# Expert columns head-innermost, choice and product in one VectorE instruction, mean of squares on GpSimd

## The chip, the core and the metric

The kernel runs on one core of a Trainium2 chip. The core has five engines that run side by side, each with its own queue in program order: TensorE (PE; PEld is its loading of weights), VectorE (DVE), ScalarE (ACT), GpSimd (POOL) and SyncE (SP), which issues DMAs here. They are held together by semaphores. The metric is the device time of one execution in microseconds, and lower is better.

## What is computed

`x` has 2 x 1024 tokens of 512 columns. After a layer norm, two attentions are computed and added to `x`.

The first ("local") has 16 query heads and 4 key/value heads of 32 columns, with biases, a norm over the 32 columns of each head and a rotary embedding; a query sees 64 keys back. The norm divides by the root of the mean of squares:

```python
rms = jnp.sqrt(jnp.mean(x * x, axis=-1, keepdims=True) + RMS_EPS)
```

The second ("routed") has 16 query heads, but one key and one value per token, chosen by a gate among 16 experts:

```python
gating = jax.nn.softmax(x @ W_gate.T, axis=-1)
idx = jnp.argmax(gating, axis=-1)
indicator = jax.nn.one_hot(idx, H, dtype=gating.dtype)
top1_val = jnp.max(gating, axis=-1, keepdims=True)
q, k, v = jnp.split(x @ W_qkv.T, 3, axis=-1)
k_shared = jnp.einsum('bth,bthd->btd', indicator, k)
v_shared = jnp.einsum('bth,bthd->btd', indicator * top1_val, v)
```

Attention over them is causal over 1024 tokens.

## The kernel before, in words

A planner (`make_plan`) writes one list of steps before the program is built, from costs and due times that it holds for each step; every engine's program walks this same list, so the order of each queue is fixed by hand. The change touches neither the planner nor its costs.

The first stage runs in 8 rounds of 256 tokens, two tiles of 128 each (`a` = 0, 1). In a round TensorE multiplies the normalised and transposed tokens with the weights, in parts: `kvg` (local key and value, and the gate's 16 columns), `q`, `fk` and `fv` (all 16 experts' keys and values, 512 columns each), and `qt` (routed queries, transposed, four chunks). Each float32 product is made of three matmuls of high and low halves. The results go to two PSUM banks in turn (`gemm`), and TensorE may use a bank again when VectorE or ScalarE has read it (`gemm_read`). The local attention of the tile before, its output projection and the first row maxima of the routed attention (`first_max`, L1292 and L1299, into `r_first`) are woven in between. All transposes but those of the probabilities go through one more bank, `tp1`. The second stage is the rest of the routed attention, eight units over k_stack and v_all.

The steps that the change touches, for one tile:

- `kv_biased` (L1172 to L1180) adds the bias and takes the gate's maximum; `g_score` is the rank where the gate equals its maximum, and 0 elsewhere. `gate_sum` takes the greatest rank (`g_rank`, L1186) and marks it (`g_hot`, L1188).
- `picked` (L1211) multiplies the 16 experts' columns, in the bank, by `g_hot`; this frees the bank. The sum over the heads (L1216) gives `chosen`, 32 columns. In the bank and in `picked` the columns lie head after head, 32 each.
- `fk_hi` (ScalarE, L1437 and L1439) copies the chosen key, rounded for the matmul, into two parts of `fk_stack[a]`, the high half twice; `fk_lo` (VectorE, L1223) makes the low half, `chosen - high`, in the third. `fk_stack` (TensorE, L965) transposes both tiles' stacks through `tp1`, and ScalarE (L1481) copies them to `k_stack`. `fv_out` (L1428) scales the chosen value.
- `qt` (ScalarE L1460, VectorE L1249) makes the high and low halves of a chunk of routed queries.
- `q_square` (ScalarE L1449) squares queries and keys of the local attention; `q_rms` sums each head's 32 squares on VectorE (`rms_t`, L1238), divides by 32 and adds epsilon there (`rms_v`, L1242), and GpSimd raises to the power -1/2 (`rms_y`, L1610). GpSimd's rotary work (L1634, L1640, L1644) goes before it, and its product with `rms_y` (L1618) after it; then TensorE transposes the queries (L949).

## Time and profile before

| | |
|---|---|
| timed runs, median of 3 | 686.83 us (685.67 to 688.93) |
| profiled execution, span | 684.4 us |
| profiled execution, its own time | not listed; the timed runs are other executions |
| TensorE busy | 646.0 us, 94% of the span |
| VectorE busy | 496.3 us, 73% |
| ScalarE busy | 362.5 us, 53% |
| GpSimd busy | 442.6 us, 65% |

The span goes from the first to the last instruction of one execution. Busy time is the time in which an engine worked on at least one instruction.

### The profile page before, as it was taken

To read this page: it belongs to the slowest core of one execution; us is meant where nothing else is said; L and a number is where in the kernel's file an instruction comes from. 1 tells how busy PE (TensorE), PEld (TensorE's weight loads), DVE (VectorE), ACT (ScalarE), POOL (GpSimd) and SP (SyncE) were. 2 spreads that over 40 slices of the span, in tenths; PEclk is the share of its full clock that TensorE was granted. 3 is DMA by queue.
4 is the path that set the end of the run, shared out by engine and by line. 5 is a ranking of instruction groups with operands and counts; after the bars stand their busy time and mean duration, and the time that the engine had idled before them with its cause. 6 is when DMAs were issued, how large, how long until landed. Compare 5 with 4: busy or idle time off the path is not lost.

```text
span 684.4 us, 19451 instructions
## 1 busy us (share of the span) xinstructions
PE 646.0 (94%) x7432; PEld 510.2 (75%) x7432; DVE 496.3 (73%) x1328; ACT 362.5 (53%) x906; POOL 442.6 (65%) x368
## 2 busy tenths in 40 slices
PE   3788999999999899999899899999999999999997
PEld 3577888887788688888688667777777777777775
DVE  3956966677678866787676368888888787879454
ACT  4436444472527344445335555556566566656674
POOL 3965764938195735684487267685868777778730
PEclk9979999999999999999999999999999999999999
DMA  8522213231232032222214541321314131402011
GB/s 295 206 59 86 82 38 115 86 98 51 66 102 61 30 112 70 64 70 74 77 32 118 158 142 56 96 64 50 111 49 110 51 106 32 110 28 87 4 33 33
DMA packets 64942, 56.61 MB, mean 83 GB/s; under 512 B 6481, under 2 KB 48849, under 8 KB 64849
## 3 DMA queue, kind: packets, MB, share of 16 engines
q1 hardware_dynamic: 62704, 54.45, 27.2%
q8 instruction: 58, 0.95, 0.6%
q10 hardware_dynamic: 2144, 0.93, 0.5%
q14 instruction: 36, 0.29, 0.1%
HBM read 37.20 MB, written 17.89 MB: 80 GB/s over the span
## 4 chain that ended last, share of the span: by engine, by line
PE 78%; DVE 9%; POOL 4%; ACT 3%; issue 2%; DMA 2%; ACTq 1%; DVEq 0%; POOLq 0%
PE gemm L938 17%; PE s_ps L1047 12%; PE od_ps L1096 11%; PE st_ps L1080 10%; PE gemm L1024 6%; PE od_ps L1110 5%; PE win L998 3%; PE gemm L934 3%; PE win L983 2%; PE s_ps L1119 2%; DMA rope_t<-rope 2%; PE av L1010 2%; DVE l_sum L1266 2%; ACT p_loc L1492 2%; DVE l_max L1257 1%
## 5 line engine op out<-in xcount | busy, mean ns | idle before, releaser
L938 PE MATMUL gemm<-w_tok,xt 128*128 128x512 f32 (+1 forms) x768 | 186.1, 384 | 3.3 <-DVE x_res L1283 0.9
L938 PEld LDWEIGHTS gemm<-w_tok,xt 128*128 128x128 f32 x768 | 131.7, 193 | 28.2 <-issue 1.4
L1318 DVE CUSTOM_DVE_ANT_0 s_ps<-s_ps,x_ln 128x512 f32<-128x512 f32 (+3 forms) x224 | 127.6, 620 | 24.4 <-PE s_ps L1047 24.0
L1047 PE MATMUL s_ps<-k_stack,w_tok 96*128 96x512 f32 (+2 forms) x336 | 101.5, 385 | 0.3 <-DVE x_res L1283 0.3
L1080 PE MATMUL st_ps<-w_tok,k_stack 98*128 98x512 f32 x288 | 99.0, 413 | 0.2 <-ACT p_loc L1540 0.2
L1540 ACT ACTIVATE p_loc<-st_ps 128x512 f32<-128x512 f32 x144 | 77.7, 599 | 36.0 <-PE st_ps L1080 34.8
L1634 POOL TENSOR_TENSOR rope_b<-qkv,sin_t 128x128 f32<-128x128 f32 (+1 forms) x32 | 27.5, 880 | 79.5 <-DVE qkv L1232 79.3
L1047 PEld LDWEIGHTS s_ps<-k_stack,w_tok 96*128 96x128 f32 x336 | 55.0, 188 | 28.3 <-DVE picked_fk L1318 12.4
L1492 ACT ACTIVATE p_loc<-win,l_max 128x96 f32<-128x96 f32 x256 | 60.9, 391 | 19.1 <-DVE l_max L1257 19.0
L934 PE MATMUL gemm<-xt,w_qt 128*128 128x256 f32 x384 | 57.1, 293 | 6.3 <-DVE picked_fv L1211 3.5
L1540 ACT ACTIVATE p_loc_t<-st_ps 128x512 f32<-128x512 f32 x96 | 52.4, 599 | 19.8 <-PE st_ps L1080 19.3
L1318 DVE CUSTOM_DVE_ANT_0 s_ps<-s_ps,x_ln,picked_fk 128x128 f32<-128x128 f32 (+3 forms) x112 | 56.8, 556 | 7.5 <-PE s_ps L1047 7.1
L1658 POOL TENSOR_TENSOR p_loc<-p_loc,l_rec 128x1536 f32<-128x1536 f32 x16 | 44.1, 2757 | 26.9 <-DVE l_rec L1269 26.9
L1610 POOL TENSOR_TENSOR rms_y<-rms_v,minus_half 128x20 f32<-128x20 f32 x16 | 58.6, 3665 | 3.3 <-DVE rms_v L1242 2.8
L934 PEld LDWEIGHTS gemm<-xt,w_qt 128*128 128x128 f32 x384 | 50.6, 194 | 10.2 <-DVE picked_fv L1211 4.5
L1024 PE MATMUL gemm<-w_o,attn_t 128*128 128x512 f32 x192 | 54.8, 414 | 3.2 <-DVE attn_t L1274 2.4
L1080 PEld LDWEIGHTS st_ps<-w_tok,k_stack 98*128 98x128 f32 x288 | 50.5, 189 | 9.0 <-ACT p_loc L1540 2.1
L1318 DVE DVE_READ_ACCUMULATOR2_ANT picked_fk<- 128x1 f32 x336 | 47.8, 142 | 0.0
L1501 ACT ACTIVATE p_loc_t<-win 96x512 f32<-96x512 f32 x64 | 36.8, 634 | 16.6 <-PE win L998 16.5
L1096 PE MATMUL od_ps<-p_loc,v_all 128*32 128x128 f32 x1152 | 44.3, 277 | 0.0
L1024 PEld LDWEIGHTS gemm<-w_o,attn_t 128*128 128x128 f32 x192 | 34.1, 193 | 10.0 <-issue 3.2
L1676 POOL TENSOR_SCALAR_AFFINE_SELECT p_loc<-p_loc 128x512 f32<-128x512 f32 x40 | 25.0, 634 | 24.8 <-ACT p_loc L1540 24.8
(172 smaller groups left out, 1298.7 us busy)
## 6 DMA issues: line engine op xcount, KB each, us to landing
w_tok<-q_parts SPq DMA_DIRECT2D x72, 128.0 KB, 2.6
q_parts<-qt SPq DMA_DIRECT2D x120, 64.0 KB
x_ln<-x SPq DMA_DIRECT2D x8, 512.0 KB, 4.7
x_res<-x SPq DMA_DIRECT2D x16, 256.0 KB, 2.9
partial<-x_res SPq DMA_DIRECT2D x16, 256.0 KB, 2.6
w_tok<-partial SPq DMA_DIRECT2D x8, 512.0 KB, 5.2
raw<-w_tok SPq DMA_DIRECT2D x3, 1024.0 KB, 12.9
v_win<-v_rows SPq DMA_DIRECT2D x64, 48.0 KB, 2.2
```

Source lines behind the costliest of these rows:

```text
L934: i = e.matmul(g[:, 0:PAIR], w_qt_p[r][:, k, a * P:(a + 1) * P], xs[l][:, k, :], start=first, stop=last)
L938: i = e.matmul(g[:, 0:cols], xs[l][:, k, a * P:(a + 1) * P], w_tok_p[r][:, k, c0:c0 + cols], start=first, stop=last)
L1024: i = e.matmul(gemm[bank][:, :], attn_t[l][:, kc, :], w_o_p[r][:, kc, :], start=kc == 0 and q == 0, stop=kc == KC - 1 and q == 2)
L1047: e.matmul(s_ps[bank][:, 0:cols], q_op[b][0:HALVES, i, h, :], k_stack[0:HALVES, b * S + c0:b * S + c0 + cols], start=True, stop=True).then ...
L1080: e.matmul(st_ps[k % ST_BANKS][:, :, :], k_stack[0:HALVES + 2, b * S + j * P:b * S + (j + 1) * P], q_op[b][0:HALVES + 2, i, :, :], start=T ...
L1096: mm = e.matmul(od_ps[h * DK:(h + 1) * DK, 0, :], v_all[:, b * IT + j, 0:DK], p_t[k % RING][:, h, :], start=i == j, stop=ends_row(k))
L1318: e.tensor_tensor_reduce(out=s[:, 0:cols], in0=s[:, 0:cols], in1=causal[:, S - width + c0:S - width + c0 + cols], scale=1.0, scalar=dst if ...
L1492: i = e.activation(p_loc[a][:, g, quad, :], win[:, g, quad * KEYS:(quad + 1) * KEYS], ACT.Exp, bias=l_max[:, a, n:n + 1])
L1501: e.activation(p_loc_t[quad][0:KEYS, :, :].rearrange("p g q -> p (g q)"), win[0:KEYS, quad, :], ACT.Copy).then_inc(*M["p_t_r"].did((m, a, ...
L1540: e.activation(p_t[k % RING][:, :, :], st_ps[k % ST_BANKS][:, :, :], ACT.Exp, scale=ROUTED_SCALE).then_inc(*M["rp_exp"].did((u, k)))
L1610: e.tensor_tensor(rms_y[:, :], rms_v[:, :], minus_half[:, :].to_broadcast([P, NH]), ALU.pow).then_inc(*M["rms_r"].did((n, a)))
L1658: e.tensor_tensor(p_l, p_l, l_rec[:, a, :].unsqueeze(2).to_broadcast([P, H, KEYS]), ALU.mult).then_inc(*M["p_r"].did((m, a)))
```

## The change

The weights of the experts' keys and values are handed over with their columns ordered column-major over heads (all 16 heads of column 0, then of column 1, and so on), so that `picked` and its sum find the 16 heads of a column side by side. `g_hot` goes: one `scalar_tensor_tensor` compares the ranks with the greatest and multiplies the bank's columns by the outcome. The chosen key lies in the fourth part of `fk_stack[a]`; ScalarE's second copy has its sign turned, and the low half is a sum of two, `chosen + (-high)`, by `tensor_reduce`; the query's low half has its sign turned as well, so that their product stays. The division by 32 and the epsilon go from VectorE to GpSimd. The list of steps stays.

```diff
-    chosen = {k: sb(one, f"chosen_{k}", [P, DK]) for k in ("fk", "fv")}
-    fk_stack = [sb(one, f"fk_stack{a}", [P, HALVES]) for a in range(2)]
+    chosen_fv = sb(one, "chosen_fv", [P, DK])
+    fk_stack = [sb(one, f"fk_stack{a}", [P, HALVES + DK]) for a in range(2)]
+    chosen = {("fv", a): chosen_fv[:, :] for a in range(2)} | {
+        ("fk", a): fk_stack[a][:, HALVES:HALVES + DK] for a in range(2)}
...
-                e.tensor_reduce(g_rank[:, a:a + 1], g_score[:, a, :], AX.X, ALU.max).then_inc(*seq.did())
-                lane.wait_ge(*seq.now())
-                e.tensor_scalar(g_hot[:, a, :], g_score[:, a, :], g_rank[:, a:a + 1], None, ALU.is_equal).then_inc(
-                    *seq.did(("hot", n, a)))
+                e.tensor_reduce(g_rank[:, a:a + 1], g_score[:, a, :], AX.X, ALU.max).then_inc(*seq.did(("rank", n, a)))
...
-                e.tensor_tensor(picked[kind][:, :].rearrange("p (h d) -> p h d", h=H),
-                                g[:, :].rearrange("p (h d) -> p h d", h=H),
-                                g_hot[:, a, :].unsqueeze(2).to_broadcast([P, H, DK]), ALU.mult).then_inc(
-                                    *M["gemm_read"].did((n, kind, a)))
+                e.scalar_tensor_tensor(picked[kind][:, :].rearrange("p (d h) -> p d h", h=H),
+                                       g_score[:, a, :].unsqueeze(1).to_broadcast([P, DK, H]), g_rank[:, a:a + 1],
+                                       g[:, :].rearrange("p (d h) -> p d h", h=H), ALU.is_equal, ALU.mult).then_inc(
+                                           *M["gemm_read"].did((n, kind, a)))
                 lane.wait_ge(*M["gemm_read"].of((n, kind, a)))
-                e.tensor_reduce(chosen[kind][:, :], picked[kind][:, :].rearrange("p (h d) -> p d h", h=H), AX.X,
+                e.tensor_reduce(chosen[kind, a], picked[kind][:, :].rearrange("p (d h) -> p d h", h=H), AX.X,
                                 ALU.add).then_inc(*M[f"picked_{kind}"].did((n, a)))
...
-                lane.wait_ge(*M["fk_hi"].of((n, a)))
-                e.tensor_tensor(dst[:, 2 * DK:3 * DK].bitcast(F32R), chosen["fk"][:, :], dst[:, 0:DK],
-                                ALU.subtract).then_inc(*M["fk_lo"].did((n, a)))
+                lane.wait_ge(*M["fk_dup"].of((n, a)))
+                chosen_and_minus_hi = dst[:, DK:4 * DK].rearrange("p (b d) -> p d b", d=DK)[:, :, ::2]
+                e.tensor_reduce(dst[:, 2 * DK:3 * DK], chosen_and_minus_hi, AX.X,
+                                ALU.add).then_inc(*M["fk_lo"].did((n, a)))
...
-                e.tensor_reduce(rms_t[:, :], rope_sq[:, :, :], AX.X, ALU.add).then_inc(*seq.did(("squares", n, a)))
-                lane.wait_ge(*seq.now())
                 if n or a:
-                    lane.wait_ge(*M["rms_r"].of(tile_before(n, a)))
-                e.tensor_scalar(rms_v[:, :], rms_t[:, :], 1.0 / DK, RMS_EPS, ALU.mult, ALU.add).then_inc(
-                    *M["rms_v_r"].did((n, a)))
+                    lane.wait_ge(*M["rms_m_r"].of(tile_before(n, a)))
+                e.tensor_reduce(rms_t[:, :], rope_sq[:, :, :], AX.X, ALU.add).then_inc(*M["rms_v_r"].did((n, a)))
...
-                e.tensor_tensor(qt_of(1, n, c), g[:, 0:PAIR], qt_of(0, n, c).bitcast(F32),
+                e.tensor_tensor(qt_of(1, n, c), qt_of(0, n, c).bitcast(F32), g[:, 0:PAIR],
                                 ALU.subtract).then_inc(*M["gemm_read"].did((n, "qt", c)))
...
-                e.activation(dst[:, 0:DK].bitcast(F32R), chosen["fk"][:, :], ACT.Copy).then_inc(
-                    *M["fk_hi"].did((n, a)))
-                e.activation(dst[:, DK:2 * DK].bitcast(F32R), chosen["fk"][:, :], ACT.Copy).then_inc(
+                e.activation(dst[:, 0:DK].bitcast(F32R), chosen["fk", a], ACT.Copy).then_inc(*M["fk_hi"].did((n, a)))
+                e.activation(dst[:, DK:2 * DK].bitcast(F32R), chosen["fk", a], ACT.Copy, scale=-1.0).then_inc(
                     *M["fk_dup"].did((n, a)))
...
+                e.tensor_scalar(rms_v[:, :], rms_t[:, :], 1.0 / DK, RMS_EPS, ALU.mult, ALU.add).then_inc(
+                    *M["rms_m_r"].did((n, a)))
+                lane.wait_ge(*M["rms_m_r"].of((n, a)))
                 e.tensor_tensor(rms_y[:, :], rms_v[:, :], minus_half[:, :].to_broadcast([P, NH]), ALU.pow).then_inc(
                     *M["rms_r"].did((n, a)))
```

## Rows read from the trace of the kernel before

**Rows 1.** The page's first line.
```profile
span 684.4 us, 19451 instructions
```

**Rows 2.** Stretches: us, busy time of each engine, granted clock, DMA share, GB/s.
```profile
20.00:40.00 20.00, 13.71 (x66) 11.24 (x66) 17.58 (x27) 5.86 (x11) 18.42 (x11) 0.81 0.35 124
60.00:180.00 120.00, 119.15 (x1087) 100.09 (x1085) 85.98 (x176) 57.86 (x178) 74.63 (x53) 1.00 0.28 83
180.00:340.00 160.00, 151.93 (x1296) 127.01 (x1297) 120.20 (x225) 72.34 (x232) 98.81 (x69) 1.00 0.25 72
400.00:684.00 284.00, 278.69 (x4336) 204.83 (x4336) 220.05 (x826) 174.44 (x355) 196.58 (x186) 1.00 0.24 66
```

**Rows 3.** TensorE's waits, 0 to 400: us in total, times, longest.
```profile
PE tp L965 <- DVE fk_stack L1223: 4.0, 4, 1.8
PE gemm L934 <- DVE picked_fv L1211: 3.5, 4, 1.6
...
PE tp L949 <- POOL qkv L1618: 1.4, 2, 1.2
```

**Rows 4.** Groups on VectorE, 0 to 400: count, busy us, mean ns, idle before.
```profile
L1216 DVE TENSOR_REDUCE chosen_fk<-picked_fk 128x32 f32<-128x512 f32 x16 | 17.5, 1094 | 0.5
...
L1238 DVE TENSOR_REDUCE rms_t<-rope_sq 128x20 f32<-128x640 f32 x16 | 12.9, 807 | 2.7 <-ACT rope_sq L1449 2.7
L1249 DVE TENSOR_TENSOR qt<-gemm,qt 128x256 fp32r<-128x256 f32 x30 | 12.5, 415 | 7.1 <-ACT qt L1460 7.1
L1223 DVE TENSOR_TENSOR fk_stack<-chosen_fk,fk_stack 128x32 fp32r<-128x32 f32 x16 | 11.5, 719 | 0.0
...
L1211 DVE TENSOR_TENSOR picked_fk<-gemm,g_hot 128x512 f32<-128x512 f32 x16 | 11.0, 685 | 2.7 <-PE gemm L938 2.5
...
L1242 DVE TENSOR_SCALAR rms_v<-rms_t 128x20 f32<-128x20 f32 x16 | 9.8, 612 | 0.6
L1188 DVE TENSOR_SCALAR g_hot<-g_score,g_rank 128x16 f32<-128x16 f32 x16 | 8.0, 499 | 0.6
...
L1180 DVE TENSOR_SCALAR g_exp<-gemm,g_max 128x16 f32<-128x16 f32 x16 | 3.6, 225 | 0.0
```

**Rows 5.** Line 1223's instructions: shortest, median, longest in ns.
```profile
L1223 DVE TENSOR_TENSOR fk_stack<-chosen_fk,fk_stack x16: 128/194/2291, 34.1 to 362.1; 128x32 fp32r<-128x32 f32 x16
```

**Rows 6.** Timeline near 236: start, duration, instruction, idle before and its releaser.
```profile
235.64 2.75 POOL L1658 TENSOR_TENSOR p_loc<-p_loc,l_rec 128x1536 f32<-128x1536 f32 x1
...
236.25 2.19 DVE L1223 TENSOR_TENSOR fk_stack<-chosen_fk,fk_stack 128x32 fp32r<-128x32 f32 x1
...
238.50 0.42 PE L965 MATMUL tp<-idt,fk_stack 128*96 128x128 f32 x2 [1.79 <-DVE fk_stack L1223]
```

**Rows 7.** Timeline of TensorE, four instructions that it came to idle.
```profile
205.00 0.96 PE L938 MATMUL gemm<-w_tok,xt 128*128 128x512 f32 x3 [0.41 <-DVE picked_fk L1211]
...
306.48 0.96 PE L934 MATMUL gemm<-xt,w_qt 128*128 128x256 f32 x6 [0.49 <-DVE picked_fv L1211]
327.46 1.08 PE L1010 MATMUL av<-p_loc_t,v_win 96*32 96x128 f32 x32 [0.97 <-DVE r_first L1299]
332.62 0.42 PE L965 MATMUL tp<-idt,fk_stack 128*96 128x128 f32 x2 [1.47 <-DVE fk_stack L1223]
```

**Rows 8.** Timeline of VectorE, in the queue ahead of two of those.
```profile
201.59 1.10 DVE L1242 TENSOR_SCALAR rms_v<-rms_t 128x20 f32<-128x20 f32 x1
...
304.98 0.85 DVE L1223 TENSOR_TENSOR fk_stack<-chosen_fk,fk_stack 128x32 fp32r<-128x32 f32 x1
```

**Rows 9.** Two groups on GpSimd, 0 to 400.
```profile
L1610 POOL TENSOR_TENSOR rms_y<-rms_v,minus_half 128x20 f32<-128x20 f32 x16 | 58.6, 3665 | 3.3 <-DVE rms_v L1242 2.8
...
L1579 POOL TENSOR_TENSOR ln_b<-ln_t,ln_y 128x2 f32<-128x2 f32 x8 | 1.6, 195 | 0.6
```

**Rows 10.** Timeline of the start, VectorE and GpSimd.
```profile
31.15 3.00 DVE L1134 TENSOR_TENSOR w_o<-raw,w_o 128x2048 fp32r<-128x2048 f32 x1
...
31.96 5.59 POOL L1610 TENSOR_TENSOR rms_y<-rms_v,minus_half 128x20 f32<-128x20 f32 x1
```

More of the change, by code:

```diff
@@ L695 @@
 MARKS = (
-    "x_in xn_r ln_seq ln_b_r ln_v_r ln_y_r rms_v_r seq "
+    "x_in xn_r ln_seq ln_b_r ln_v_r ln_y_r rms_v_r rms_m_r seq "
     "xt_mm xt_hi xt_lo gemm_mm gemm_read kv_r sq_r rms_r rope_ab rope_sum rope_r "
@@ L771, in mixed_attention_kernel @@
     r_first = sb(one, "r_first", [P, IT, HQ])
-    g_exp, g_score, g_hot = (sb(one, n, [P, 2, H]) for n in ("g_exp", "g_score", "g_hot"))
+    g_exp, g_score = (sb(one, n, [P, 2, H]) for n in ("g_exp", "g_score"))
     over = ExitStack()
@@ L964, in tensor_program @@
                 for a in range(2):
-                    i = e.transpose(tp1[0:HALVES, a, :], fk_stack[a][:, :], idt[:, :])
+                    i = e.transpose(tp1[0:HALVES, a, :], fk_stack[a][:, 0:HALVES], idt[:, :])
                 i.then_inc(*M["fk_mm"].did(m))
@@ L1201, in vector_program @@
                 lane.wait_ge(*M["gemm_mm"].of((n, kind, a)))
-                lane.wait_ge(*seq.of(("hot", n, a)))
+                lane.wait_ge(*seq.of(("rank", n, a)))
                 if a or n:
@@ L1427, in scalar_program @@
                     lane.wait_ge(*filled_all())
-                e.activation(v_all[:, 2 * n + a:2 * n + a + 1, 0:DK], chosen["fv"][:, :].unsqueeze(1), ACT.Copy,
+                e.activation(v_all[:, 2 * n + a:2 * n + a + 1, 0:DK], chosen["fv", a].unsqueeze(1), ACT.Copy,
                              scale=g_top[:, a:a + 1]).then_inc(*M["fv_out"].did((n, a)))
@@ L1558, in seq_squares @@
     def seq_squares(n, a):
-        return M["seq"].of(("squares", *tile_before(n, a)))
+        return M["rms_v_r"].of(tile_before(n, a))
     def gpsimd_program(e):
@@ L1879, in heads, with by_column @@
         return w.reshape(-1, DK, *w.shape[1:])[:, even_first].reshape(w.shape)
+    def by_column(w):
+        return w.reshape(H, DK, D).swapaxes(0, 1).reshape(w.shape)
     def by_rep(w):
@@ L1888 @@
         "x": a["L0_attn_x"].reshape(TOK, D),
-        "w_tok": np.concatenate([wq, wk, a["L0_attn_Wv"], a["L0_ffn_W_gate"], fk, fv], 0).T,
+        "w_tok": np.concatenate([wq, wk, a["L0_attn_Wv"], a["L0_ffn_W_gate"], by_column(fk),
+                                 by_column(fv)], 0).T,
         "w_qt": fq.T,
```

## The prediction

> **What bounds the kernel now.** I read first how the span divides. The profiled execution spans 684.4 us [rows 1]; the three timed runs have a median of 686.83, 2.4 more, and since no time of the profiled execution itself is listed I make the sum on its span and carry the difference in microseconds over to the median. The stretches [rows 2] come next. TensorE is busy 119.15 of 120 us in 60 to 180 and 278.69 of 284 from 400 on, but 151.93 of 160 in 180 to 340 (8.07 idle), and 13.71 of 20 in 20 to 40. VectorE, where nearly all of the edit lies, is busy 86 of 120 and 120 of 160. So TensorE sets the pace; VectorE matters only where TensorE stands still for it. The edit touches the first stage alone, which ends near 400, so it can win no more than TensorE's idle time there.
>
> Second, whom TensorE waits for in that stage [rows 3]: 4.0 us in four stalls for the key's low half (L1223), 3.5 for the release of a bank by `picked_fv`, 1.4 in two stalls for the query tile that GpSimd scales last (L1618). Third, the groups of VectorE [rows 4] and the spread of one of them [rows 5]: the low half, 32 columns, has a median of 194 ns and a maximum of 2291. Fourth, why: at 236.25 it takes 2.19 us, and it ends, at 238.44, as GpSimd's 2.75 us `scaled` ends at 238.39; TensorE's transposes then start at 238.50 after 1.79 us idle [rows 6]. An instruction with two operands from SBUF was held until GpSimd's finished, and the profile counts the hold in its duration.
>
> **The change part by part.**
>
> *The sum over heads.* Now 1094 ns for 512 elements read 32 words apart [rows 4], 32 times (`fk` and `fv`). The other sum with neighbours side by side, `rms_t`, needs 807 ns for 640. Two VectorE products, 685 ns for 512 columns and 415 for 256, give 1.055 ns a column, so `rms_t` has 132 ns fixed, and a sum of 512 neighbours should take 132 + 540 = 672. Saved 0.42 us each, 13.4 us of VectorE in all. The bounds are 0 (if the 32 short results and not the distance are the cost) and 0.42. I take 0.42: `rms_t` has 20 results and shows no cost for them.
> The Trainium skill (Vector Engine (DVE) Microarchitecture Reference, 5.2 Measured stream behaviour on trn2) gives 0.65 cycle for each element that hops. By that rule the sum would save about 0.35 us, an estimate, and the whole forecast would be 0.2 us less. The row says 0.82 ns an element.
>
> *Choice and product in one.* It removes `g_hot`, 499 ns, 16 times: 8.0 us. The product keeps its 512 columns but takes a per-row scalar. `g_exp` has one and costs 225 ns for 16 columns, 208 fixed, where the plain product has 145 fixed. So 0.75 instead of 0.685, or 0.065 more, 32 times, 2.1 us. Bounds: 0.685 (the scalar is free) and 1.094 (the gate row that is read over and over walks like the strided sum). The row is 16 neighbours long, so I take 0.75. The bank comes free 0.065 later, counted from where the instruction starts.
>
> *Key's low half.* 719 ns on average now [rows 4]. As a sum of two over 32 pairs it has 64 elements: 132 + 68 ns, and 0.82 ns more for each hop, 52, so 0.25 us; bounds 0.13 (the least that the product took [rows 5] was 0.128) and 0.28. It has one source and should not be held. Saved 0.47 x 16 = 7.5 us. It now waits for the second ScalarE copy too, a copy of 32 columns behind the first; in the held cases both copies had long ended. The sign turned in the query's low half changes no count or shape.
>
> *Mean of squares to GpSimd.* VectorE loses 612 ns x 16 = 9.8 us. GpSimd gains an instruction on 20 columns between `rope`'s last sum and the power. The nearest row on GpSimd is `ln_b`, 195 ns for 2 columns [rows 9]; with 18 columns more and the wait for its own result I take 0.3 us, a guess between the bounds 0.2 (that row) and 0.61 (what the instruction took on VectorE), nearer to the first because the engine is the same. Where GpSimd stood waiting for VectorE's step it gets part of this back.
>
> VectorE sheds 13.4 + 8.0 + 7.5 + 9.8 - 2.1 = 36.6 us of busy time. Nearly all of it lies beside TensorE's work and is worth nothing. What counts are the stalls, one by one:
> - The low half's four stalls, 4.0 us [rows 3]: 1.79 at 238.50, 1.47 at 332.62 [rows 6, 7] vanish. Of the other two, 0.7 together, I count 0.5: they stand behind a queue of VectorE with shortened sums in it, not behind a hold. Sum 3.75.
> - `picked_fk` at 205.00, 0.41 [rows 7]: a held mean of squares, 1.10 us, stood in the queue before it [rows 8]; all goes. `picked_fv` at 306.48, 0.49: it started when a held low half, 0.85 us, ended [rows 8]; all goes. `r_first` at 327.46, 0.97: a strided sum of `fk` stands right in front; 0.42 goes. Sum 1.3.
> - Not gained: `x_res` and transposed `x` stalls, where VectorE had stood idle in front and only the longest reduction of local scores is in the way, and the stalls behind ScalarE.
> - The start. TensorE waits up to 1.2 us for the first query tile from GpSimd [rows 3], whose power took 5.59 us there because VectorE's weight subtraction, 3.00 us from 31.15, held it [rows 10]; the group's mean is 3.67 [rows 9]. VectorE gets there sooner, but the subtraction holds GpSimd just as long, now in the instruction before. So what TensorE waits for VectorE before that (the 1.6 us that is the longest of `picked_fv` [rows 3]) only moves behind, to the same wait for GpSimd, and the mean adds 0.35. The second stall for that result gets 0.3 longer. Cost 0.65.
>
> Sum: -3.75 - 1.3 + 0.65 = -4.4 us, to 680.0 in the span and 686.83 - 4.4 = 682.4 in the median.
>
> **The clock.** TensorE's granted clock is 0.81 of full in 20 to 40 [rows 2], so part of that stretch ran at the lower level (1.2 GHz), where TensorE was busy 13.71 of 20 us. Since the start keeps its idle time, only in another order, I leave it at nothing; the matmuls there can move by 2 us either way.
>
> **The rivals.**
> *A. The stalls are taken up by others.* TensorE arrives earlier at the transposes behind ScalarE's copies and at GpSimd's `rope`. For it: GpSimd's result came too late twice already [rows 3]. Against: that is 2 of 16 tiles. If only the two large low-half stalls go and half is given back: -1.6, 685.2.
> *B. More goes than I traced.* A VectorE queue 36.6 us shorter releases banks sooner everywhere. All of TensorE's 8.07 + 0.85 us idle in 60 to 340 gone [rows 2]: -9 us, 677.8. Against: several of these waits had VectorE idle before them.
> *C. GpSimd becomes the bound.* This ends slower. The mean is on the way to `q_t` in each of 16 tiles. If each paid 0.61 us and TensorE waited every time: -5.05 + 9.8 = +4.7, 691.6. It decides from 0.53 us a tile ((5.05 + 3.4) / 16). Against it: TensorE waited for this result only twice, 1.4 us in all [rows 3].
> The Trainium skill (GPSIMD Engine Reference, 8. Key points) says that elementwise work is about twice as fast on VectorE; by that alone the step would be dearer where it goes.
> *D. The fused product is slow.* At 1.09 us it eats the shortened sum, 0.41 x 32 = 13 us, and releases the bank later: four bank stalls grow by 0.34 more, two queues lose their shortened sum (0.25 and 0.42), and the result is -4.4 + 1.4 + 0.7 = -2.3, 684.5.
>
> **How the numbers follow.** Chances: forecast 0.55, A 0.20, B 0.15, C 0.06, D 0.04. No change that a measurement of this kernel can tell is within 0.5%, 3.4 us, so faster means under 683.4. My own case has 1 us to spare: three quarters of it are faster. Faster 0.42 + 0.15 = 0.57; same 0.13 + 0.20 + 0.04 = 0.37; slower 0.06. The range reaches to B below, 677.8, and above past A to 686.5, 0.3 us short of nothing gained at all. Outside lie C, half of B and the outer part of A: 0.06 + 0.08 + 0.05.
>
> **What the new profile would show.** `chosen` near 0.67 us, the fused `picked` near 0.75, the low half near 0.25 with no maximum over 0.4, no `g_hot`, a new GpSimd group under 0.3. VectorE busy near 460 us. In TensorE's waits the line for `fk_stack` nearly gone, L949 behind GpSimd near 2 us, and 180 to 340 with TensorE busy in all but about 3.5 us of its (shorter) stretch. Wrong would be: a new name at the head of TensorE's waits (A, C), a `picked` over 1 us (D), or a second spell at the lower clock outside the start and the end of the first stage.

## The result and the profile after

The changed kernel takes 680.69 us (median of 5, 680.16 to 682.2) against 686.72 for the kernel before (5 runs beside it): a ratio of 0.9919, 95% interval 0.9897 to 0.994. That is 6.0 us less, where 4.4 less was forecast, and the spans of the profiled executions say the same: 678.1 against 684.4 [rows 1]. The profiled execution's own time is 680.16.

The page's first lines, and the stretches of time: us, busy time of each engine with its count, granted clock, share of DMA, GB/s.

```profile
span 678.1 us, 19434 instructions
...
PE 641.4 (95%) x7432; PEld 508.8 (75%) x7432; DVE 461.8 (68%) x1296; ACT 362.7 (53%) x906; POOL 446.2 (66%) x384
```

```profile
20.00:40.00 20.00, 11.63 (x64) 9.04 (x63) 15.06 (x26) 6.19 (x11) 18.97 (x13) 0.99 0.41 137
40.00:60.00 20.00, 17.63 (x124) 15.08 (x124) 10.38 (x18) 9.95 (x31) 11.19 (x11) 0.84 0.14 38
60.00:180.00 120.00, 118.63 (x1085) 99.86 (x1084) 76.25 (x165) 58.48 (x179) 76.02 (x58) 1.00 0.27 83
180.00:340.00 160.00, 156.60 (x1337) 132.05 (x1336) 107.02 (x214) 77.46 (x248) 100.61 (x77) 1.00 0.25 75
340.00:400.00 60.00, 55.37 (x521) 44.73 (x522) 30.79 (x67) 30.67 (x84) 40.45 (x33) 1.00 0.46 125
```

The gain is where TensorE stood still before: 180 to 340 has 3.4 us without TensorE, where it had 8.07 [rows 2]. The start is not better. TensorE works 11.63 us of 20 to 40, not 13.71, though at a clock of 0.99 instead of 0.81, and the lower level (1.2 GHz) has moved behind it, to 40 to 60 at 0.84.

TensorE's waits from 0 to 400 (total, times, longest):

```profile
PE tp L951 <- POOL qkv L1617: 4.8, 2, 4.3
PE gemm L936 <- DVE picked_fv L1210: 3.9, 3, 2.4
...
PE av L1012 <- DVE r_first L1296: 0.7, 2, 0.6
```

TensorE waits for `fk_stack` nowhere in this stretch any more; before, that was 4.0 us in four stalls [rows 3]. The wait for GpSimd's query tile stands in its place, with 4.3 us at one stroke and 4.8 in all, where near 2 was forecast; the timelines below show that this is mostly the old wait at the start under another name.

Groups on VectorE and the two of GpSimd's power (count, busy us, mean ns, idle before), and the spread of the low half in ns:

```profile
L1210 DVE SCALAR_TENSOR_TENSOR picked_fk<-g_score,g_rank,gemm 128x512 f32<-128x512 f32 x16 | 11.9, 742 | 4.0 <-PE gemm L940 3.8
...
L1215 DVE TENSOR_REDUCE fk_stack<-picked_fk 128x32 f32<-128x512 f32 x16 | 11.0, 686 | 0.5
...
L1223 DVE TENSOR_REDUCE fk_stack<-fk_stack 128x32 f32<-128x64 f32 x16 | 3.3, 205 | 0.0
```

```profile
L1609 POOL TENSOR_TENSOR rms_y<-rms_v,minus_half 128x20 f32<-128x20 f32 x16 | 56.6, 3537 | 1.3
...
L1606 POOL TENSOR_SCALAR rms_v<-rms_t 128x20 f32<-128x20 f32 x16 | 3.3, 208 | 2.6 <-DVE rms_t L1240 1.5
```

```profile
L1223 DVE TENSOR_REDUCE fk_stack<-fk_stack x16: 160/212/217, 32.9 to 357.8; 128x32 f32<-128x64 f32 x16
```

Every price was met: the sum 686 ns (672 forecast), the fused product 742 (750), the low half 205 with a maximum of 217 (250, none over 400), the mean 208 (300). VectorE is busy 461.8 us (460 forecast).

The place of the first long stall, in the timeline of VectorE, GpSimd and TensorE:

```profile
237.01 0.21 DVE L1223 TENSOR_REDUCE fk_stack<-fk_stack 128x32 f32<-128x64 f32 x1
...
237.01 2.76 POOL L1657 TENSOR_TENSOR p_loc<-p_loc,l_rec 128x1536 f32<-128x1536 f32 x1
...
237.71 0.38 PE L967 MATMUL tp<-idt,fk_stack 128*96 128x128 f32 x2
```

GpSimd's long instruction runs as before, the low half takes 0.21 us beside it, and TensorE's transposes have no idle time in front [rows 6]. But look at the starts: both were issued at 237.01. Before, the low half came 0.61 us behind. At the second place (327.64 against 327.86) it is even ahead. So this trace does not tell whether the low half is fast because it has one source, or because it is no longer behind. That question led the experiments.

The start, on GpSimd and then TensorE:

```profile
30.88 3.55 POOL L1643 TENSOR_TENSOR qkv<-qkv,rope_b 128x640 f32<-128x640 f32 x1
34.51 0.21 POOL L1606 TENSOR_SCALAR rms_v<-rms_t 128x20 f32<-128x20 f32 x1
34.81 3.54 POOL L1609 TENSOR_TENSOR rms_y<-rms_v,minus_half 128x20 f32<-128x20 f32 x1
38.49 1.26 POOL L1617 TENSOR_TENSOR qkv<-qkv,rms_y 128x640 f32<-128x640 f32 x1
```

```profile
39.81 1.11 PE L951 MATMUL tp<-idt,qkv 128*128 128x128 f32 x4 [4.30 <-POOL qkv L1617]
...
56.66 1.01 PE L936 MATMUL gemm<-xt,w_qt 128*128 128x256 f32 x3 [2.37 <-DVE picked_fv L1210]
```

As forecast, the weights' subtraction (VectorE, 30.74 to 33.02) now holds `rope`'s last sum, 3.55 us here against a group mean of 1.69, instead of the power [rows 10]. The mean and its hand-off put 0.30 us (34.51 to 34.81) on the path to the first query tile.

Both programs issue the same 7432 matmuls in the same order, so one matmul's start can be compared with its own start in the other kernel. This shows where each microsecond went:

| matmul | before | after | after minus before |
|---|---|---|---|
| first query tile | 39.01 | 39.81 | +0.8 |
| behind `picked_fv` at the start | 56.00 | 56.66 | +0.7 |
| third query tile | 77.65 | 80.07 | +2.4 |
| behind `picked_fk` | 205.00 | 206.43 | +1.4 |
| first `fk_stack` place | 238.50 | 237.71 | -0.8 |
| behind `picked_fv` | 306.48 | 304.80 | -1.7 |
| first maxima | 327.46 | 324.82 | -2.6 |
| second `fk_stack` place | 332.62 | 328.36 | -4.3 |
| behind `attn_t`, near the end of the first stage | 386.13 | 381.86 | -4.3 |
| 5 us later | 390.84 | 384.95 | -5.9 |
| last round of the second stage | 666.18 | 659.86 | -6.3 |

### The profile page after: what moved, and what is told of

The parts are those of the page before. It is cut to its first block, busy times and chain, and to the rows that moved or that the text cites. A ratio compares the mean times of both kernels' runs of the same rounds, so it can differ in the third digit from the quotient of the medians.

```text
span 678.1 us, 19434 instructions
## 1 busy us (share of the span) xinstructions
PE 641.4 (95%) x7432; PEld 508.8 (75%) x7432; DVE 461.8 (68%) x1296; ACT 362.7 (53%) x906; POOL 446.2 (66%) x384
## 4 chain that ended last, share of the span: by engine, by line
PE 83%; POOL 5%; DVE 4%; ACT 3%; DMA 2%; issue 2%; ACTq 1%; DVEq 0%; POOLq 0%
PE gemm L940 19%; PE s_ps L1049 12%; PE od_ps L1098 11%; PE st_ps L1082 10%; PE gemm L1026 6%; PE od_ps L1112 5%; PE gemm L936 5%; PE win L1000 3%; PE win L985 3%; PE s_ps L1121 2%; DMA rope_t<-rope 2%; PE av L1012 2%; ACT p_loc L1488 2%; PE tp L951 1%; DVE l_max L1254 1%
## 5 line engine op out<-in xcount | busy, mean ns | idle before, releaser
L1609 POOL TENSOR_TENSOR rms_y<-rms_v,minus_half 128x20 f32<-128x20 f32 x16 | 56.6, 3537 | 1.3
```

The costliest lines, as they stand in the source:

```text
L1609: e.tensor_tensor(rms_y[:, :], rms_v[:, :], minus_half[:, :].to_broadcast([P, NH]), ALU.pow).then_inc(*M["rms_r"].did((n, a)))
```

## The experiments

Three sets, each on one chip beside runs of the kernel before. Ratios are to the kernel before of the same set, with 95% intervals. The diffs show the lines that matter; `...` marks what is left out.

**First set: what does each part give back when it is undone?** The low half with two sources again, everything else as in the changed kernel:

```diff
-                chosen_and_minus_hi = dst[:, DK:4 * DK].rearrange("p (b d) -> p d b", d=DK)[:, :, ::2]
-                e.tensor_reduce(dst[:, 2 * DK:3 * DK], chosen_and_minus_hi, AX.X,
+                e.tensor_tensor(dst[:, 2 * DK:3 * DK], dst[:, 3 * DK:4 * DK], dst[:, DK:2 * DK],
                                 ALU.add).then_inc(*M["fk_lo"].did((n, a)))
```

> The changed kernel, but the key's low half is again a product-type instruction with two operands from SBUF (chosen + minus high); same waits, layout and place. Theory H (holds: such an instruction is held while GpSimd works, and the few places where TensorE stands behind it are the gain): the longest comes back to 2 us or more, the stalls of TensorE at L965-type transposes come back with 3 to 4 us, median near 684.2. Rival P (proportional: each us of VectorE time shed gives the same 0.16 us, 5.6 of 34.5): VectorE gains about 8 us, so 1.3 us, median near 682.0.

Measured: 679.48 us, 0.9906 (0.9885 to 0.9927). Nothing was lost. The timeline at the place of the long stall (VectorE, GpSimd, TensorE):

```profile
235.10 0.18 DVE L1222 TENSOR_TENSOR fk_stack<-fk_stack 128x32 f32<-128x32 f32 x1
...
235.11 2.80 POOL L1656 TENSOR_TENSOR p_loc<-p_loc,l_rec 128x1536 f32<-128x1536 f32 x1
...
235.81 0.38 PE L967 MATMUL tp<-idt,fk_stack 128*96 128x128 f32 x2
```

The two-source instruction was issued 0.01 us ahead of GpSimd's and took 0.18. At the second place it came 0.21 ahead and took 0.30. Elsewhere it was still held, up to 1.52 us, but TensorE did not wait. (That it took 0.30 there is the tail of another instruction: GpSimd's product before it, L1616, ended at 326.02 and the low half at 326.06.) So in the changed kernel the form of the low half is worth nothing, and my reason for the gain seemed to fall.

The sum over heads strided again (expert columns head after head, and no reordering of the weights), the rest as changed:

```diff
-                e.tensor_reduce(chosen[kind, a], picked[kind][:, :].rearrange("p (d h) -> p d h", h=H), AX.X,
+                e.tensor_reduce(chosen[kind, a], picked[kind][:, :].rearrange("p (h d) -> p d h", h=H), AX.X,
...
```

> The changed kernel with the experts' columns head after head again: the fused product stays, the sum over heads walks 32 words apart. Theory H: the sum is back at 1.09 us, VectorE 13 us busier, but only the stalls with a shortened sum right in front come back (0.25 + 0.42 and a little), median near 681.6. Rival P: 13 x 0.16 = 2.1, median 682.8. If the distance is not what made it slow, the sum stays at 0.69.

Measured: 682.82 us, 0.9951 (0.9934 to 0.9969), against 0.9906 of the run above in the same set. The sum takes 1096 and 1084 ns again, and 3.3 us are lost against that run (the intervals are apart). That run differs in the low half's form too; against the changed kernel itself (0.9919) it is 2.2 us, with intervals that just overlap. The median is nearer to the rival's number (682.8) than to my sum (681.6).

The division and epsilon back on VectorE:

```diff
+                e.tensor_reduce(rms_t[:, :], rope_sq[:, :, :], AX.X, ALU.add).then_inc(*M["rms_v_r"].did((n, a)))
+                lane.wait_ge(*M["rms_v_r"].of((n, a)))
                 if n or a:
...
+                    lane.wait_ge(*M["rms_r"].of(tile_before(n, a)))
+                e.tensor_scalar(rms_v[:, :], rms_t[:, :], 1.0 / DK, RMS_EPS, ALU.mult, ALU.add).then_inc(
+                    *M["rms_m_r"].did((n, a)))
...
```

> The changed kernel with the division by 32 and the epsilon on VectorE again, as a tensor_scalar that can be held. Theory H: the 0.3 us on GpSimd's way to the first query tile and to that near 80 go (-0.6), the stall at picked_fk near 205 comes back (+0.4), median 680.5, within 0.5 of the changed kernel. Rival P: 9.8 us more VectorE, +1.6, 682.3. Rival C (GpSimd's way to the query tiles is the bound): 16 x 0.3 less, 4.8, median near 676.

Measured: 678.42 us, 0.9894 (0.987 to 0.9918): no slower than the changed kernel (680.5 was expected). The low half is issued 0.29 us behind GpSimd's instruction again and still takes 0.22:

```profile
235.19 2.76 POOL L1657 TENSOR_TENSOR p_loc<-p_loc,l_rec 128x1536 f32<-128x1536 f32 x1
...
235.48 0.22 DVE L1223 TENSOR_REDUCE fk_stack<-fk_stack 128x32 f32<-128x64 f32 x1
```

Being behind does not hold the one-source form.

The last subtraction of weights (`w_o`, 2.28 us on VectorE) done only when GpSimd has scaled the first query tile (`rope_r`):

```diff
+LATE_BEFORE = ("qt", 0, 1)
...
-            if step == "w_lo":
-                n, = key
+            if step == "w_lo" and key[0] == len(PIECES) - 1:
+                continue
+
+            if step == "w_lo" or (step, *key) == LATE_BEFORE:
+                n = key[0] if step == "w_lo" else len(PIECES) - 1
...
+                if step != "w_lo":
+                    lane.wait_ge(*M["rope_r"].of((0, 0)))
...
```

> The changed kernel with VectorE's last weight subtraction (2.3 us, two operands from SBUF) moved behind the first query tile's scaling on GpSimd, where GpSimd stands idle. Theory H: GpSimd's rotary sum there falls from 3.55 to 1.55 us, the first query tile comes 2.0 us sooner, and TensorE's stall of 4.3 us before it falls to about 2.3; median near 678.7. Rival S (the start is given back at the second tile, which waits for ScalarE's exponentials): the start's gain is eaten before 60 us, median 680.7.

Measured: 679.06 us, 0.9897 (0.9879 to 0.9916). GpSimd's sum takes 1.57 us instead of 3.55, and the first query tile's transposes start at 37.07 instead of 39.81, but only about 1.6 us is left in the total against the changed kernel, with intervals that overlap.

**Second set: each part alone on the kernel before.** The low half as a sum of two, with the two signs and the place of the chosen key that belong to it, and nothing else of the change:

```diff
-                lane.wait_ge(*M["fk_hi"].of((n, a)))
-                e.tensor_tensor(dst[:, 2 * DK:3 * DK].bitcast(F32R), chosen["fk"][:, :], dst[:, 0:DK],
-                                ALU.subtract).then_inc(*M["fk_lo"].did((n, a)))
+                lane.wait_ge(*M["fk_dup"].of((n, a)))
+                e.tensor_reduce(dst[:, 2 * DK:3 * DK], chosen_and_minus_hi, AX.X,
+                                ALU.add).then_inc(*M["fk_lo"].did((n, a)))
```

> The kernel before with only the key's low half changed to the sum of two (and the two signs turned, chosen key in the stack). Theory R (race for the port: the product form is held only where GpSimd's scaling of the local weights starts just before it; in the kernel before it does so twice with TensorE waiting behind): both long stalls go whole, 3.3 us, and 0.3 elsewhere; ratio 0.9948. Rival P (each us of VectorE time is worth 0.16 us): 8 us less, 1.3 us, ratio 0.998.

Measured: 680.13 us, 0.9911 (0.9891 to 0.9931). This one part alone measures as much as the whole change, and more than the 0.9948 that I expected, which lies outside the interval. Its low half is issued 0.56 us behind GpSimd's instruction, just where it was held before:

```profile
234.08 2.76 POOL L1660 TENSOR_TENSOR p_loc<-p_loc,l_rec 128x1536 f32<-128x1536 f32 x1
...
234.64 0.21 DVE L1226 TENSOR_REDUCE fk_stack<-fk_stack 128x32 f32<-128x64 f32 x1
...
234.93 0.40 PE L967 MATMUL tp<-idt,fk_stack 128*96 128x128 f32 x2
```

The shorter sum alone (columns head-innermost, two instructions for choice and product as before):

```diff
...
-                e.tensor_reduce(chosen[kind][:, :], picked[kind][:, :].rearrange("p (h d) -> p d h", h=H), AX.X,
+                e.tensor_reduce(chosen[kind][:, :], picked[kind][:, :].rearrange("p (d h) -> p d h", h=H), AX.X,
...
```

> The kernel before with only the experts' columns head-innermost: product with g_hot and sum, both with neighbours side by side. Theory R: the sum falls to 0.69; at the stall near 238 the low half is issued at about 235.84, still after GpSimd's scaling (235.64), so that hold stays; near 330 it comes within 0.1 us of it, either way; 1.0 us goes at other stalls. Together 1.0 to 2.5 us, ratio 0.9965 to 0.9985. Rival P: 13.4 x 0.16 = 2.1, ratio 0.997. What tells them apart is the low half's longest time near 238: over 2 us by R.

Measured: 685.57 us, 0.9997 (0.9981 to 1.0012). The sum is 686 ns, 0.41 less, 32 times, and none of it arrives in the time, though 1.0 to 2.5 us were expected. At the first long stall:

```profile
234.69 2.76 POOL L1658 TENSOR_TENSOR p_loc<-p_loc,l_rec 128x1536 f32<-128x1536 f32 x1
...
234.90 2.59 DVE L1223 TENSOR_TENSOR fk_stack<-chosen_fk,fk_stack 128x32 fp32r<-128x32 f32 x1
...
237.55 0.42 PE L965 MATMUL tp<-idt,fk_stack 128*96 128x128 f32 x2 [1.78 <-DVE fk_stack L1223]
```

The low half gets there 0.4 us sooner than before, 0.21 behind and not 0.61, and is held 0.4 us longer, 2.59 and not 2.19 [rows 6]. Held work ends when the holder ends; what is saved in front of it is spent in the hold. That is not the whole of it. Elsewhere this profile does gain: at 327 us its matmuls are 2.1 us ahead of the kernel before. The second long stall, 1.78 us and not 1.47, takes 0.4 of that, and the clock, which falls to the lower level 1.4 us behind this stall, takes 1.5.

Both the strided sum and the two-source low half put back into the changed kernel, so that the fused product and the mean on GpSimd are what is left of the change:

```diff
-                e.tensor_reduce(chosen[kind, a], picked[kind][:, :].rearrange("p (d h) -> p d h", h=H), AX.X,
+                e.tensor_reduce(chosen[kind, a], picked[kind][:, :].rearrange("p (h d) -> p d h", h=H), AX.X,
...
-                e.tensor_reduce(dst[:, 2 * DK:3 * DK], chosen_and_minus_hi, AX.X,
+                e.tensor_tensor(dst[:, 2 * DK:3 * DK], dst[:, 3 * DK:4 * DK], dst[:, DK:2 * DK],
...
```

> The changed kernel with both undone: the strided sum and the two-source low half. Undone singly, the low half cost nothing and the sum 2.2 us. Theory R: with the strided sum the low half is issued 0.2 to 0.4 us after GpSimd's scaling again, is held over 2 us near 240 and 330, and both TensorE stalls return: 3.5 us more than with the strided sum alone, ratio near 1.000. Rival P or plain addition: 0.9951, as with the strided sum alone, plus at most 1.3 us of VectorE's (0.997).

Measured: 688.33 us, 1.0034 (1.0019 to 1.0048). The low half is issued 0.41 us behind `scaled` and takes 2.39, and TensorE stands 2.00 us; at the second place it stands 1.74. Both times the clock falls behind the stall, at 241.28 and 336.85, and the matmuls lose 1.5 to 1.6 us more there; so more comes back than the 3.5 us expected.

The late weight subtraction together with the mean on VectorE (both diffs of the first set; shown here is GpSimd's side of the mean):

```diff
-                e.tensor_scalar(rms_v[:, :], rms_t[:, :], 1.0 / DK, RMS_EPS, ALU.mult, ALU.add).then_inc(
-                    *M["rms_m_r"].did((n, a)))
-                lane.wait_ge(*M["rms_m_r"].of((n, a)))
```

> The changed kernel with the last weight subtraction behind the first query tile's scaling, and the division by 32 back on VectorE. Theory: late subtraction gives 2.0 us at the start, the mean off GpSimd's way 0.6 there and at the third tile, and costs 0.4 near 205; against the kernel before a ratio of 0.987, 677.5. Rival S (the second tile waits for ScalarE's exponentials, which wait for the first query tile, so the start's gain stays; but the held mean comes back in the queue at 49 us): 0.990.

Measured: 676.21 us (4 runs), 0.9853 (0.9832 to 0.9875), the fastest of all. It is the changed kernel without its last part and with 2.28 us of VectorE moved out of GpSimd's way. The first query tile starts at 37.51.

**Third set: is it a race?** The first set had spoken against the low half and the second for it. A race would explain both: the two-source form is held only when it is issued behind GpSimd's `scaled`, and in the changed kernel the shorter sum and the mean on GpSimd together let it be first. This kernel is the changed one with the two-source low half, and the mean back on VectorE:

```diff
-                e.tensor_reduce(dst[:, 2 * DK:3 * DK], chosen_and_minus_hi, AX.X,
+                e.tensor_tensor(dst[:, 2 * DK:3 * DK], dst[:, 3 * DK:4 * DK], dst[:, DK:2 * DK],
...
+                e.tensor_scalar(rms_v[:, :], rms_t[:, :], 1.0 / DK, RMS_EPS, ALU.mult, ALU.add).then_inc(
+                    *M["rms_m_r"].did((n, a)))
```

> The changed kernel with the two-source low half and the mean of squares on VectorE; sum and fused product stay as changed. Undone singly, neither cost anything (0.991 and 0.989). Theory R: without the mean GpSimd's scaling starts 0.3 us sooner; with the mean on VectorE the low half came at 235.48 after the scaling at 235.19, and at 326.35 after 326.15, so the product form is held there over 2 us both times, and 3.3 us or more come back: ratio 0.994 to 0.998. Addition of the single results: 0.989 to 0.991.

Measured: 684.84 us, 0.9977 (0.9961 to 0.9994). Line 1222's spread and who waited, then the three instructions:

```profile
L1222 DVE TENSOR_TENSOR fk_stack<-fk_stack x16: 128/194/2608, 33.6 to 360.3; 128x32 f32<-128x32 f32 x16
...
  PE tp L967: 3.4, 2
```

```profile
234.58 2.75 POOL L1656 TENSOR_TENSOR p_loc<-p_loc,l_rec 128x1536 f32<-128x1536 f32 x1
...
234.86 2.52 DVE L1222 TENSOR_TENSOR fk_stack<-fk_stack 128x32 f32<-128x32 f32 x1
```

Both long stalls are back, 3.4 us in two. The same two-source form that lost nothing beside the mean on GpSimd loses 0.9977 - 0.9894 = 0.8% without it.

The mean alone on GpSimd, on the kernel before:

```diff
...
                     lane.wait_ge(*M["rope_r"].of(tile_before(n, a)))
+                e.tensor_scalar(rms_v[:, :], rms_t[:, :], 1.0 / DK, RMS_EPS, ALU.mult, ALU.add).then_inc(
+                    *M["rms_m_r"].did((n, a)))
+                lane.wait_ge(*M["rms_m_r"].of((n, a)))
```

> The kernel before with only the division by 32 and the epsilon on GpSimd. Theory R: GpSimd's scaling near 235.6 starts 0.3 us later, but the low half there came 0.6 us after it, so the hold and the stall stay, 0.3 us shorter; the start and the third tile pay 0.65; the stall at 205 goes. Sum -0.4 us, ratio 0.998 to 1.001. Rival P (9.8 us of VectorE at 0.16): 0.9977. Rival C (GpSimd's way is the bound, 0.3 a tile): +4.8 us, 1.007.

Measured: 688.11 us, 1.0033 (1.002 to 1.0047): slower, and outside the 0.998 to 1.001 expected. The low half comes 0.36 us behind (0.13 at the second place), so the race isn't won, and TensorE stands 2.04 and 1.85 us. The clock falls 1.4 us behind the first and 2.1 us behind the second. The windows (columns as above):

```profile
228.00:240.00 12.00, 9.87 (x76) 7.65 (x74) 9.85 (x15) 1.21 (x4) 11.47 (x8) 1.00 0.08 29
240.00:250.00 10.00, 9.67 (x90) 8.48 (x91) 4.46 (x12) 3.29 (x12) 1.35 (x2) 0.83 0.58 164
325.00:335.00 10.00, 7.26 (x72) 6.05 (x70) 9.60 (x13) 2.27 (x7) 9.29 (x6) 1.00 0.04 12
335.00:345.00 10.00, 9.37 (x82) 7.72 (x83) 4.06 (x11) 3.09 (x12) 1.19 (x1) 0.83 0.35 95
```

Between 240 and 242, this kernel's matmuls fall from 1.7 us behind those of the kernel before to 3.2 behind, so such a fall costs 1.5 us beside its stall.

The changed kernel with GpSimd's new instruction three times instead of once:

```diff
                 e.tensor_scalar(rms_v[:, :], rms_t[:, :], 1.0 / DK, RMS_EPS, ALU.mult, ALU.add).then_inc(
+                    *M["rms_m_r"].did())
+                lane.wait_ge(*M["rms_m_r"].now())
+                e.tensor_scalar(rms_v[:, :], rms_t[:, :], 1.0 / DK, RMS_EPS, ALU.mult, ALU.add).then_inc(
+                    *M["rms_m_r"].did())
+                lane.wait_ge(*M["rms_m_r"].now())
+                e.tensor_scalar(rms_v[:, :], rms_t[:, :], 1.0 / DK, RMS_EPS, ALU.mult, ALU.add).then_inc(
```

> The changed kernel with the small GpSimd instruction (division and epsilon) carried out three times in a row, each waiting for the one before: about 0.6 us more on GpSimd's way to each query tile; the output is the same. My sum: only the first query tile and the third pay, 1.2 us, and 0.3 where the tile near 289 had no slack; ratio 0.9940. Rival C (every tile pays): 16 x 0.6 = 9.6 us, 1.006.

Measured: 683.43 us, 0.9967 (0.9955 to 0.9978). Two more of 0.21 us and a 0.08 us hand-off, 16 times, are 9.3 us on GpSimd; some 3 us of it arrive, where 1.5 at most were expected: about 1.6 by the third query tile (81.68 against 80.07), the rest between 100 and 290 us.

## Why the prediction was right, and where not

**The low half.** Forecast: -3.75 us, because one source isn't held. This is the main cause, and it is shown. Four pairs of kernels, each alike but for the low half's form (in the first row its signs and the place of the chosen key change with it):

| | two sources | one source |
|---|---|---|
| strided sum, mean on VectorE (the kernel before) | 1 | 0.9911 |
| strided sum, mean on GpSimd, fused product | 1.0034 | 0.9951 |
| short sum, mean on VectorE, fused product | 0.9977 | 0.9894 |
| short sum, mean on GpSimd, fused product | 0.9906 | 0.9919 |

In three rows one source is worth 0.8 to 0.9%, some 6 us; in the fourth nothing (the intervals overlap). How far behind GpSimd's `scaled` (the 2.76 us that scale `p_loc`) the two-source low half was issued, at the two places, explains it:

| kernel | first, second place, us behind | low half took, us |
|---|---|---|
| before | 0.61, 0.51 | 2.19, 2.29 |
| sum alone | 0.21, 0.14 | 2.59, 2.67 |
| mean alone | 0.36, 0.13 | 2.44, 2.67 |
| mean and fused product | 0.41, 0.20 | 2.39, 2.61 |
| sum and fused product | 0.28, 0.19 | 2.52, 2.61 |
| sum, mean and fused product | -0.01, -0.21 | 0.18, 0.30 |

The shorter sum brings the low half 0.40 us forward (0.61 to 0.21), the mean puts `scaled` 0.25 back (0.61 to 0.36); either alone is not enough for 0.61, both are, by a hair. The Trainium skill (SBUF — State Buffer, Who interferes with whom) says that a VectorE instruction with two SBUF inputs contends with a GpSimd instruction that reads SBUF, that the ports they share are an exclusive lock for which issue order decides who blocks, and that `tensor_reduce` never contends on this chip. These rows agree, from 0.01 us ahead (0.18 us) to 0.13 behind (2.67 us). Behind GpSimd's power, though, which reads SBUF too, the two-source low half was held in no kernel. In the kernel before, seven were issued 0.17 to 3.1 us behind it, while it ran, and took 174 to 202 ns; one of them:

```profile
119.47 3.53 POOL L1610 TENSOR_TENSOR rms_y<-rms_v,minus_half 128x20 f32<-128x20 f32 x1 [0.87 <-DVE rms_v L1242]
...
119.64 0.18 DVE L1223 TENSOR_TENSOR fk_stack<-chosen_fk,fk_stack 128x32 fp32r<-128x32 f32 x1
```

There the measurement decides; no run shows why it differs.

So "should not be held" came out right: in no kernel did the one-source form take longer than 223 ns, and at these places it was issued up to 0.56 us behind. The reason given, one source, was too wide: `rms_v` too has one source, and was held 1.10 us [rows 8]. What holds here is that `tensor_reduce` with one source isn't held. And the prediction did not see that the other parts together would also have removed the two long stalls, without margin.

Its size is nearly right where no clock is in play. From before to the low half alone, the same matmuls gain 4.5 us between the third query tile and 380 us. The prediction counted 3.75 here, and 0.49 more for the `picked_fv` stall at 306.48 under another heading, though with this cause; 4.24 together. The same stretch gives 4.4 us for the third pair of the table (neither has a fall of the clock there), and 7.1 us for the second, where the clock falls behind both stalls. The timed 6 us lie between; that the clock makes up the difference fits these traces but isn't shown for the timed executions. In the one profile of the low half alone, 1.6 us more come from the start, where the lower level ends at 34 us and not at 43, which the low half does not explain.

**The sum over heads.** Its price was right (686 ns, 672 forecast, 0.41 saved). The rule of the Trainium skill that the prediction cites (Vector Engine (DVE) Microarchitecture Reference, 5.2 Measured stream behaviour on trn2) would have had it save about 0.35; here each hop cost (1094 - 686) / 512 = 0.80 ns, and the measurement decides. Its worth was forecast as 1.3 us of stalls. Of the three stalls named, the `picked_fk` and `picked_fv` ones are gone, and `r_first` fell from 0.97 to 0.57, 0.40 for a forecast 0.42. But the first two have other causes, a held mean and a held low half, as the prediction itself says, so they don't speak for the sum: at the `picked_fv` stall 0.6 us are gained with the low half alone, too. On the changed kernel the strided sum costs 1.7 us between the third query tile and 380 us, and 2.2 in the time (0.9951 against 0.9919; 3.3 against the changed kernel with two sources). Alone on the kernel before it is worth 0 in the time (0.9981 to 1.0012): the hold swallows what is saved ahead of it, and in the profiled execution the clock took most of the rest. So this term was right, under a condition that the prediction did not state.

**The mean on GpSimd.** The instruction is cheaper than forecast (0.30 with hand-off, 0.35 forecast), yet the term +0.65 at the start came out as +2.4 at the third query tile, and what is missing in it is the clock. The mean alone does it as well (79.99 against 77.65, +2.3), the mean on VectorE doesn't (77.95). The table of matmuls shows where it arises. The matmul at 56.66 is 0.7 us late, much as the first query tile was (0.8); 0.30 of that is the mean with its hand-off, and the rest stood before it (GpSimd's rotary sum starts at 30.88, and at 30.46 in the kernel before). TensorE stands 2.37 us there for the bank that `picked_fv` frees, where it stood 1.29:

```profile
56.00 1.31 PE L934 MATMUL gemm<-xt,w_qt 128*128 128x256 f32 x9 [1.29 <-DVE picked_fv L1211]
```

The stall ends 0.7 us later, like what came ahead of it, and begins 0.4 sooner (54.30, before 54.71). In the kernel before, a held mean stood on VectorE (48.95, 1.29 us); with it gone the work ahead is done sooner. But ScalarE sets the end: VectorE sits idle 3.51 us in front, behind ScalarE's copy of the transposed tokens, which stands behind its 3.8 us of exponentials. At the end of this longer stall the clock falls (56.59), as the row above at 0.84 shows. In the seven kernels with the mean on GpSimd this stall is 2.3 to 2.4 us, and in six the lower level follows; in the six with it on VectorE it is 1.3 to 1.7 us, and it never does. From this stall's end to the third query tile, 20 us on, five kernels with the fall lose 1.8 us against the kernel before (2.4 with three means); the one without it, the late subtraction, loses 0.2; and the five others with the mean on VectorE differ from it by less than 0.1. So the instruction itself costs about 0.2 here (0.3 forecast), and the fall 1.6, which the prediction had at nothing. Why the clock did not fall in the seventh kernel is open, with one profile of each. In the steady stretch the mean gives some back: up to 380 us the changed kernel gains 6.7 us and its undoing 5.9, with 0.6 of that at 205, the stall that the prediction traced to the held mean. In time the mean costs 0.3% alone (1.002 to 1.0047) and 0.4% beside the fastest kernel (0.9897 with it, 0.9853 without, intervals apart); between the changed kernel and its undoing (0.9919, 0.9894) it can't be told.

**The fused product.** 742 ns as forecast. The kernel with it and the mean (1.0034) and that with the mean alone (1.0033) are equal, within 0.15% either way: it is hidden, and so is the `g_hot` that it saves.

**The clock.** "I leave it at nothing; the matmuls there can move by 2 us either way" was no price at all, and of all steps of the prediction this one failed. Its reason, that the start keeps its idle time, did not hold: the stall before 56.66 grew by 1.1 us. Two effects cancelled in the total. One is the fall behind 56.66, 1.6 us. The other is near 390. In the profiled before, the clock is 0.76 between 385 and 392, behind a wait for `attn_t`, and 1.00 there after, though TensorE waits as long (1.53 us, 381.86); this gains 1.6 us between 386 and 391:

```profile
386.13 0.93 PE L1024 MATMUL gemm<-w_o,attn_t 128*128 128x512 f32 x3 [1.53 <-DVE attn_t L1274]
```

All 13 profiled kernels have this wait. In nine the lower level begins within 1.7 us of its end, in two 9 us after, and in two not before the very end of the kernel (past 675): the changed kernel and the one with its two-source low half. Two near relatives of these (three means; the late subtraction) have the fall, so that the gain is the change's is not shown; it may be luck. It nearly makes good the 1.8 us by which the start came out worse than forecast.

Over all timed executions the mean granted clock is 0.985 and 0.987 in the two slowest kernels (mean and fused product; mean alone), 0.991 in the kernel before, and 0.994 and 0.995 in the low half alone and the fastest. Of the ten long stalls (1.47 to 2.04 us) in the five profiled kernels where the low half was held, five were followed by the lower level within 2.1 us (2.04, 2.00, 1.85, 1.78 and 1.74 us); five were not (1.79, 1.78, twice 1.72, and 1.47). In the eight kernels without a hold there was no fall between 180 and 340.

**The rivals.** A (the stalls are taken up by others): no, 180 to 340 has 3.4 us idle, 3.5 forecast. B (more goes than was traced): in small part, since the steady stretch gained 6.7 us and not 5.05; but the longest idle time left in it is behind `x_res` (0.91), as argued. C (GpSimd becomes the bound): no, three means in place of one cost 3 us and not 9.3; but the mean is the part that costs. D (a slow fused product): no, 742 ns.

The sum made over: the steady stretch, 78 to 380 us, -6.7 (-5.05 forecast), of which -4.5 as with the low half alone, so that the other three parts gave 2.2 where 0.8 was counted; the start +2.4 (+0.65 forecast), 1.6 of it the clock; the clock near 390 -1.6 (0 forecast); other -0.4: -6.3 in the span. The forecast 682.4 against 680.69 measured is 1.7 us off. The main mechanism was right, and the stalls gave a third more than was counted. That the total came this close is partly luck, since the two terms of the clock, +1.6 and -1.6, cancel.

## What to carry to other kernels

Where an instruction's longest time is many times its median, ask what held it, and count time saved ahead of it as nothing until the hold is gone; give it a form that isn't held, rather than trust that it will be issued first. An experiment that undoes one part of a change can find nothing because two other parts cover for it, so undo parts in pairs or do each alone before a cause is struck off. Moving a small step to another engine for the sake of a busy share costs what it adds to the path at the start, where TensorE has little other work. And work done sooner ahead of a wait whose end is set elsewhere only makes the wait longer; here such a wait came with a fall of the clock that cost more than the step.

## What the runs showed of the hardware

- The hold behind GpSimd's 2.76 us `tensor_tensor` on 1536 columns turns on 0.14 us of order: two-source, 32 columns, 0.18 us when issued 0.01 us ahead (the changed kernel with two sources), 2.67 us when issued 0.13 us behind (the mean alone). Behind GpSimd's power on 20 columns, 3.53 us, there was none: 184 ns when issued 0.17 us behind (119.64 in the kernel before).
- The hold appears in the duration of the held instruction, not as idle time: the page's mean for `fk_stack` was 719 ns against a median of 194 [rows 4, 5].
- The same 20-column step with two immediates takes 208 ns on GpSimd, and on VectorE 0.18 us when nothing holds it and up to 1.30 us beside GpSimd's rotary sum (both in the kernels with it on VectorE), though it has one source; its group mean was 612 ns [rows 4].
- A spell at the lower clock level behind a stall cost 1.5 to 1.6 us of TensorE's time where it was read off. The stall's length alone did not tell whether it came: it followed 6 of the 7 stalls of 2.3 to 2.4 us at 53 to 58 us, 5 of the 10 of 1.47 to 2.04 us at the low half, and 9 of the 13 of 1.53 us at `attn_t`.
